# Idle products of ones ahead of product 0, and the second direction's buckets, counts and ranks spread over products 5 to 15

## The reference

```python
x = x + gnn(layernorm(x), src, dst, edge_type)     # x: 625 x 512
x = x + moe(layernorm(x))

def gnn(input, heads, tails, rel):                  # W_rel: 16 x 512 x 512
    h_self = input @ W_self.T + b_self
    H_all = einsum('rod,nd->rno', W_rel, input) + b_rel[:, None, :]
    agg = segment_sum(H_all[rel, tails], heads) + segment_sum(H_all[rel + 8, heads], tails)
    return relu(h_self + agg)

def moe(x):                                         # gate, up: 16 x 512 x 1024, down: 16 x 1024 x 512
    top_vals, top_idx = top_k(x @ router_w.T, 2)
    # per expert: (silu(x @ gate) * (x @ up)) @ down, weighted by the softmax of top_vals
```

## Time and profile before

| what | value |
|---|---|
| median of 3 runs | 710.33 us (709.69 to 710.6) |
| profiled execution, its own time | 708.9 us |
| its span, first to last instruction | 706.7 us |
| TensorE busy in the span | 683.2 us, 97% |
| VectorE busy | 607.1 us, 86% |
| ScalarE busy | 499.5 us, 71% |
| GpSimd busy | 293.1 us, 41% |
| mean granted TensorE clock | 0.994 |

### The profile page before, as it was taken

The page is one execution under the profiler, slowest core; times in us unless marked ns, Lnnn a source line. Parts: engine busy times, 40 slices in busy tenths (PEclk is TensorE's granted clock), DMA queues, the critical chain, the costliest instruction groups (busy, mean ns, idle before and its releaser), DMA issues. The chain is left out here.

```text
span 706.7 us, 10496 instructions
## 1 busy us (share of the span) xinstructions
PE 683.2 (97%) x3196; PEld 541.4 (77%) x3196; DVE 607.1 (86%) x1193; ACT 499.5 (71%) x712; POOL 293.1 (41%) x255
## 2 busy tenths in 40 slices
PE   4899999999999999999998989999999999999996
PEld 4677777777777777787766867888888888888884
DVE  8789979998999777775766989999998999999982
ACT  5645458775777777777556759888887877887881
POOL 3000037874777777757750034332231322333301
PEclk9999999999999999999998999999999999999999
DMA  7358579897999999986779699999999999999952
GB/s 254 111 164 277 149 224 333 289 286 252 317 282 301 306 308 303 303 293 210 211 214 328 257 346 403 406 405 395 407 364 406 373 374 377 359 387 376 354 190 31
DMA packets 60170, 210.69 MB, mean 298 GB/s; under 512 B 9325, under 2 KB 9722, under 8 KB 47070
## 3 DMA queue, kind: packets, MB, share of 16 engines
q1 hardware_dynamic: 41534, 154.43, 58.2%
q0 software_dynamic: 18592, 55.73, 27.4%
HBM read 181.83 MB, written 28.29 MB: 297 GB/s over the span
## 5 line engine op out<-in xcount | busy, mean ns | idle before, releaser
L416 POOL DMA_INDIRECT rows_sb<-h_dram,row_of x180 | 201.8, 1121 | 156.6 <-DVE row_of L574 89.2
L584 DVE TENSOR_TENSOR rows_lo<-rows_sb,rows_hi 128x512 fp32r<-128x512 f32 x165 | 112.8, 684 | 31.6 <-ACT rows_hi L728 31.4
L871 PE MATMUL p_h<-g_hi_sb,xt_hi_whole 128*125 128x512 f32 x320 | 128.4, 401 | 0.8 <-DVE xt_lo_whole L501 0.5
L872 PE MATMUL p_h<-g_lo_sb,xt_hi_whole 128*125 128x512 f32 x320 | 126.9, 396 | 0.0
L873 PE MATMUL p_h<-g_hi_sb,xt_lo_whole 128*125 128x512 f32 x320 | 126.7, 396 | 0.0
L728 ACT CAST rows_hi<-rows_sb 128x512 fp32r<-128x512 f32 x165 | 97.5, 617 | 22.4 <-DMA rows_sb<-h_dram,row_of 21.2
L715 ACT COPY h_whole<-p_h 125x512 f32<-125x512 f32 x80 | 46.8, 585 | 81.8 <-PE p_h L873 77.6
L1250 POOL DMA_INDIRECT tokens<-token_dram,rows_of_tokens x15 | 21.2, 1416 | 173.9 <-ACT rows_of_tokens L1556 133.8
L1304 DVE TENSOR_TENSOR u_lo_sb<-stage_up,u_hi_sb 128x2048 fp32r<-128x2048 f32 x34 | 76.4, 2285 | 1.1
L1304 DVE TENSOR_TENSOR d_lo_sb<-stage_down,d_hi_sb 128x2048 fp32r<-128x2048 f32 x32 | 71.9, 2287 | 3.7 <-ACT d_hi_sb L1541 3.7
L1678 PE MATMUL p_gate<-g_hi_sb,xt_lo_whole 128*128 128x512 f32 x256 | 74.1, 400 | 0.0
(11 more groups left out here) (308 smaller groups left out, 1304.2 us busy)
## 6 DMA issues: line engine op xcount, KB each, us to landing
stage_up<-in_L_ffn_up_w SPq DMA_DIRECT2D x34, 1024.0 KB, 8.7
stage_gate<-in_L_ffn_gate_w SPq DMA_DIRECT2D x32, 1024.0 KB, 8.7
stage_down<-in_L_ffn_down_w SPq DMA_DIRECT2D x32, 1024.0 KB, 8.4
h_dram<-h_whole SPq DMA_DIRECT2D x80, 256.0 KB, 4.1
stage_up<-in_L_gnn_W_rel SPq DMA_DIRECT2D x64, 256.0 KB, 5.5
x_whole<-in_biases SPq DMA_DIRECT2D x16, 256.0 KB, 6.4
rows_sb<-h_dram,row_of POOLq DMA_INDIRECT x180, 5.2
stage_gate<-in_L_ffn_down_w SPq DMA_DIRECT2D x2, 1024.0 KB, 10.1
```

Of the source, the lines that this page charges most:

```text
L416: q.indirect_dma_start(rows_sb[:, b % ROWS], None, h_dram[0:1 + made(n) * P], bass.IndirectOffsetOnAxis(ap=row_of[:, column_of[b]:column_o ...
L584: v.tensor_tensor(rows_lo[:, b % PARTS], rows_sb[:, b % ROWS], rows_hi[:, b % PARTS].bitcast(F32), ALU.subtract).then_inc(part_lo, 1)
L871: m.matmul(o, xt_hi[:, dc, at], wt_hi_sb[:, 1 - j % 2, dc], start=(by_matmul and dc == 0), stop=False, skip_group_check=True)
L872: m.matmul(o, xt_hi[:, dc, at], wt_lo_sb[:, 1 - j % 2, dc], start=False, stop=False, skip_group_check=True)
```

## The change

It does five things.

1. A function `keep_going(n)` issues n matmuls of the 128 by 128 tile of ones with itself into a bank of `p_h` that nobody reads before product 1 overwrites it. Five stand in the first block, seven ahead of `totals_of(0)`, two behind `ranks(0)` and three behind `turn_x(1)`.
2. `turn_x(2)`, `turn_x(3)` and `turn_x(4)` stand inside products 1, 2 and 3, behind the second of the four pieces, instead of inside products 1 and 2 behind the third and after product 2.
3. ScalarE takes the bias and the later tiles' roots earlier, VectorE the bias, tile 2's statistics and product 1's operands.
4. Direction 1's steps move: on VectorE `buckets_of(1)` and `bucket_hots(1)` from behind `scales(1)` to behind `places(0)`, `totals_of(1)` into product 7, `spans_begin` from 3 to 9, `ranks(1)` from 5 to 12, `ranks(2)` from 7 to 15; on TensorE `totals_of(1)` behind product 5, the counts behind 8, `ranks(1)` behind 10, `ranks(2)` behind 13. Totals and counts get columns in `p_sum` in place of `p_list`.
5. The marks move from products 10 to 14 to products 16 to 20.

```diff
--- before.py
+++ after.py
@@ -47,6 +47,7 @@
 LISTS = ((5, 5.5), (25, 3))
 
 LAG, START, PACE = 4, 25, 3.0
+MARKS = 16
 
 LAST_HOTS, ROUTER = 56, 72
 LOW, BIASES = 32, 2 * R + 1
@@ -263,8 +264,8 @@
             p_logits = p_list[0:TP, 0:T * NX].rearrange("p (t e) -> p t e", t=T)
             p_router = p_list[:, 256:256 + NX]
             p_ranks = p_sum[:, 0:3]
-            p_totals = [p_list[0:EC, 0:2 * T], p_list[0:EC, 2 * T:BUCKETS]]
-            p_counts = p_list[0:EXTRA + 1, 128:128 + BUCKETS]
+            p_totals = [p_list[0:EC, 0:2 * T], p_sum[0:EC, 4, 0:BUCKETS - 2 * T]]
+            p_counts = p_sum[0:EXTRA + 1, 3, 0:BUCKETS]
 
 
             PARTS_OF = ((0, 0, 2), (1, 2, 5), (1, 5, 6))
@@ -319,6 +320,11 @@
             def token_columns(a, t):
 
                 return a[:, :, t * TP:(t + 1) * TP]
+
+            def keep_going(n):
+
+                for _ in range(n):
+                    nc.tensor.matmul(p_h[:, 1, 0:P], ones[:], ones[:], start=True, stop=True)
 
             def turned(t):
                 return p_sum[:, 3 + t % 2, 0:KC * TP].rearrange("p (c n) -> p c n", c=KC)
@@ -617,42 +623,43 @@
                 normal(1)
                 scales(0)
                 scales(1)
-                buckets_of(1)
-                bucket_hots(1)
+                dve.wait_ge(bias_hi, 1)
+                v.tensor_tensor(bias_parts[LOW:LOW + BIASES], bias_f[LOW:LOW + BIASES], bias_parts[LOW:LOW + BIASES].bitcast(F32),
+                                ALU.subtract).then_inc(bias_ready, 1)
+                dve.wait_ge(rest_loaded, 16)
+                normal(2)
                 low_columns(0)
                 for dc in range(KC):
                     w_rest(0, dc)
                 low_columns(1)
-                dve.wait_ge(bias_hi, 1)
-                v.tensor_tensor(bias_parts[LOW:LOW + BIASES], bias_f[LOW:LOW + BIASES], bias_parts[LOW:LOW + BIASES].bitcast(F32),
-                                ALU.subtract).then_inc(bias_ready, 1)
-                totals_of(1)
-                dve.wait_ge(rest_loaded, 16)
-                normal(2)
                 scales(2)
                 normal(3)
+                ranks(0)
                 scales(3)
                 low_columns(2)
-                ranks(0)
                 normal(4)
                 low_columns(3)
                 scales(4)
                 told_of(0)
-                dve.wait_ge(ranks_taken, 1)
-                places(0)
                 low_columns(4)
                 for dc in range(KC):
                     w_rest(1, dc)
+                dve.wait_ge(ranks_taken, 1)
+                places(0)
+                buckets_of(1)
+                bucket_hots(1)
                 dve.wait_ge(edge_consts, 2)
                 for i in range(PRODUCTS):
                     j, t = i // T, i % T
                     if j and t:
                         w_rest(j + 1, t - 1)
-                    if i == 3:
+                    if i == 7:
+                        totals_of(1)
+                    if i == 9:
                         spans_begin()
-                    if i == 5:
+                    if i == 12:
                         ranks(1)
-                    if i == 7:
+                    if i == 15:
                         ranks(2)
                         dve.wait_ge(ranks_taken, 3)
                         then(v.tensor_tensor(place_in[:, 1], place_in[:, 1], rank_part[:], ALU.max))
@@ -756,21 +763,21 @@
                     s.activation(rstd[:, t:t + 1], rstd[:, t:t + 1], ACT.Sqrt).then_inc(root_ready, 1)
 
                 first_root(0)
+                act.wait_ge(bias_loaded, 16)
+                s.copy(bias_parts[:], bias_f[:]).then_inc(bias_hi, 1)
                 first_root(1)
                 scaled(0)
                 scaled(1)
                 turned_high(0)
+                first_root(2)
                 for dc in range(KC):
                     w_main(0, dc)
                 turned_high(1)
-                act.wait_ge(bias_loaded, 16)
-                s.copy(bias_parts[:], bias_f[:]).then_inc(bias_hi, 1)
-                take(0)
-                first_root(2)
                 scaled(2)
                 first_root(3)
+                take(0)
+                bias_in(2)
                 turned_high(2)
-                bias_in(2)
                 scaled(3)
                 take(1)
                 bias_in(3)
@@ -794,8 +801,8 @@
                     take(i)
                     if i + 2 < PRODUCTS:
                         bias_in(i + 2)
-                    if 10 <= i < 10 + T:
-                        carry_in(i - 10)
+                    if MARKS <= i < MARKS + T:
+                        carry_in(i - MARKS)
                     for b in blocks[PARTS - 3:]:
                         message(b)
                 act.wait_ge(gate_loaded, 32)
@@ -872,7 +879,7 @@
                         m.matmul(o, xt_hi[:, dc, at], wt_lo_sb[:, 1 - j % 2, dc], start=False, stop=False, skip_group_check=True)
                         last = m.matmul(o, xt_lo[:, dc, at], wt_hi_sb[:, 1 - j % 2, dc], start=False, stop=False,
                                         skip_group_check=True)
-                        if dc == KC - 2 and turned is not None:
+                        if dc == 1 and turned is not None:
                             turn_x(turned)
                     if i == 0:
                         pe.wait_ge(bias_ready, 1)
@@ -943,24 +950,28 @@
                     if t == T - 1:
                         i.then_inc(self_done, 1)
 
+                keep_going(7)
                 totals_of(0)
                 pe.wait_ge(totals_ready, 1)
                 ranks(0)
+                keep_going(2)
                 turn_x(0)
                 turn_x(1)
-                totals_of(1)
+                keep_going(3)
                 for i in range(PRODUCTS):
-                    if 10 <= i < 10 + T:
-                        mark(i - 10)
-                    product(i, i + 1 if i in (1, 2) else None)
-                    if i == 2:
+                    if MARKS <= i < MARKS + T:
+                        mark(i - MARKS)
+                    product(i, i + 1 if i in (1, 2, 3) else None)
+                    if i == 5:
+                        pe.wait_ge(xt_ready, T)
+                        totals_of(1)
+                    if i == 8:
                         pe.wait_ge(totals_ready, 2)
                         m.matmul(p_counts, ones16[0:EC, 0:EXTRA + 1], totals[0:EC], start=True, stop=True).then_inc(counts_full, 1)
-                        turn_x(4)
-                    if i == 4:
+                    if i == 10:
                         pe.wait_ge(totals_ready, 5)
                         ranks(1)
-                    if i == 6:
+                    if i == 13:
                         ranks(2)
                     for d in range(2):
                         for n in chunks(d, i):
@@ -1022,6 +1033,11 @@
                     q.tensor_tensor(select[:], ident[:, 0:BIASES], ident[:, LOW:LOW + BIASES], ALU.add)
                     q.tensor_scalar(big16[:], ident[0:EP, 0:EP], BIG, None, ALU.mult).then_inc(consts_ready, 1)
                     pool.wait_ge(consts_ready, 4)
+
+                @block.tensor
+                def _(pe):
+                    pe.wait_ge(consts_ready, 2)
+                    keep_going(5)
 
                 @block.scalar
                 def _(act):
```

## The result

| | before | after |
|---|---|---|
| median of 13 executions each | 710.33 us (708.08 to 711.27) | 708.65 us (706.92 to 710.69) |
| profiled execution, its own time | 708.9 us | 708.17 us |
| its span | 706.7 us | 706.1 us |

The ratio after to before is 0.9976, 95% interval 0.9965 to 0.9988: 1.7 us faster. The forecast was 707.0 (706.0 to 710.5): right in sign, inside the range, 1.65 us too hopeful. The two profiled executions differ by only 0.7 us, less than the medians do, and both numbers need an explanation.

The account below looks back on a forecast made before the run. TensorE, busy every microsecond from 100 to 300 us, paces the rest; its first 30 us are loose. 5.15 - 0.65 - 0.9 - 0.05 - 0.1 = 3.45, less 0.2: 3.3 us off the median 710.33, so 707.0 (706.0 to 710.5).

Parts of the forecast that it names:

- case-B: Start-up: clock rises between ranks(0) and product 0; gain 2.4 to 1.5 us, time 707.9 to 708.8; chance 0.22.
- case C: Start-up: idle products don't raise the clock before product 0; nothing gained, 710.4 us; chance 0.25.
- case A: Start-up: clock high from ranks(0) on, product 0 starts at 13.9; 3.3 us gained, 707.0 us; chance 0.45.
- the weights' landing: ScalarE's weight casts before product 0: the last weight piece may land late, up to 0.5 us; 0.2 taken off.
- my other bound: Length of one idle product at the low clock by the transposes' spacing: 0.48 us, not the 0.43 taken.
- the five in the first block: First five idle products, ending at about 4.25 us: cost 0 to 0.3 us, taken as 0.05.
- the seven are covered: Seven idle products from 4.6 to 7.6 us, before the buckets TensorE waits for until 7.91: no cost.
- no wait is left ahead of `turn_x(4)`: Products 2 and 3: tile 4 is normalised at 24.65, before turn_x(4) at 24.95; waits of 0.55 and 1.82 us go.
- ScalarE holds product 4: TensorE idles 1.7 us ahead of product 4 for ScalarE's p_h copy; product 4 starts at 28.4.
- VectorE the totals: Behind product 5, totals_of(1) waits 0.65 us for VectorE's buckets, done at 34.7.
- rival D: Products 7 to 15: VectorE late for the list, slower; 1.5 us beyond its lead gives 712; chance 0.08.
- Found again at 300 us: Dense part: the 3 us gained at product 6 should still be there at 300 us, or the prediction is wrong.

Follow-up runs that it names:

- e3: Kernel before with only the 17 idle products added, in the old order of steps; 709.68 us, ratio 0.9984.
- e11: Changed kernel with product 4's bias earlier on ScalarE, totals_of(1) behind product 6, and no idle products ahead of product 0; 707.22 us, ratio 0.9958.
- e9: Changed kernel with product 4's bias earlier, no two idle products behind ranks(0), totals_of(1) behind product 6; 706.92 us, ratio 0.9955 (5 executions).
- e2: Changed kernel without its 17 idle products ahead of product 0; 708.55 us, ratio 0.9975.
- e1: Control: changed kernel with only the waits on the number of rounds written as constants; 708.29 us, ratio 0.9963.
- e5: Changed kernel with fourteen more idle products around the last router logits, between the layers; 709.77 us, ratio 0.9999.
- e10: Control again: changed kernel with only the waits on rounds as constants, run beside e9; 708.57 us, ratio 0.9974 (9 executions).
- e7: Changed kernel with TensorE's totals_of(1) behind product 6 instead of 5; 706.97 us, ratio 0.9975.
- e8: Same kernel as e9, an earlier set of executions; 706.33 us, ratio 0.9949.
- e6: Changed kernel without the two idle products behind ranks(0); 707.95 us, ratio 0.9973.
- e4: Changed kernel with ScalarE's take(2) and bias_in(4) ahead of relation 1's last two weight casts; 708.7 us, ratio 0.9972.
- e12: Kernel before with only the four waits on the number of rounds written as constants; 709.74 us, ratio 0.9994.

## Why the forecast came out as it did

**The sign was right; how much of it the idle products earn is open.** They go with an earlier rise of the clock: product 0 takes 3.08 to 3.37 us in all ten traces with them, and 4.57, 4.64, 4.68 and 3.10 in the four without. Where product 0 would otherwise run at the low clock, they are worth 1.1 to 2.1 us at product 25 in the old order (e3's 102.20 against 103.34 and 104.30) and 1.56 in the new one (e11 against e9). Where it would not, as in e2's trace, they cost: product 25 starts at 101.23 there, and at 101.80 to 102.01 in the case-B traces with all 17. In the times only e3 shows them alone (1.15 us). In the new order, without them (e2), 1.83 of the 2.26 us that e1 gains by the means are left, while case C had "nothing" for the new order at the low clock. Either e2's executions mostly have the early rise, or C was priced too low; no trace has the changed order alone with a slow product 0.

**The step that failed is the chance of case A.** I gave A 0.45, B 0.22 and C 0.25. Of the four traces that run the changed kernel up to the layers' boundary (after, e1, e5, e10), one is A and three are B; with all kernels that hold idle products, four of ten are A (e1, e3, e7, e8), six are B, none is C. B was priced at a gain of 2.4 to 1.5, with product 0 at 14.8 if the clock is up right behind `ranks(0)` and at 15.6 if it rises only at the last three idle products. In the trace after, it is up by the transposes, but the two idle products ahead of them still take 0.99 us; product 0 starts at 15.42, and the lead at product 25 is 1.45, 1.33 and 1.54, about the lower end. B was the commoner case, and 708.8 its upper number; the median is 708.65. That the two agree so well is in part luck: the forecast let the lead reach the end whole, and in the trace after only 0.6 of 1.45 us does. The rule of the Trainium skill that I had cited with C (TensorE: Matmul & The Clock Gate, Part 1, the point of the rise varies between runs) deserved more: the traces agree with it, `ranks(0)` taking 2.51 us in one execution and 1.32 in another.

**Case A itself was about 0.5 too large.** e1 leads by 2.73 us at product 25, where the sum was 3.25 with 0.2 kept back for the weights' landing. The weights cost nothing: ScalarE's casts begin at 12.65 without a wait. The 0.2 goes elsewhere: VectorE's first `w_rest` begins at 13.29, as forecast, but product 0, which it releases, starts at 14.12 instead of 13.9. Product 4 starts at 29.06 instead of 28.4: VectorE's `scales(4)` stands behind `low_columns(3)`, which itself waits for ScalarE until 23.38, so tile 4 is normalised at 25.2 instead of 24.65. I had that chain 0.4 too short.

**An idle product** takes 0.495 us at the low clock and 0.22 at the high one (three in 0.67, from 373.48 to 374.15 in e5). I had taken 0.43 for the low clock; my other bound, 0.48 by the transposes, was the better one. That is 0.99 instead of 0.86 for the two, and e6 shows that 0.64 of it delays product 0 in case B.

**Right as written:** the five in the first block cost 0.05 (`ranks(0)` at 9.10 instead of 9.05); the seven are covered; no wait is left ahead of `turn_x(4)`; ScalarE holds product 4 and VectorE the totals; `totals_of(1)` costs 0.82 us (0.9 forecast); rival D, VectorE late for the list, is not there: no wait for a list chunk in the trace after. e4 shows how near VectorE is: one microsecond more of lead turns into a wait of 1.8 for its buckets, and in that execution the clock falls.

**"Found again at 300 us" held mostly, but not to the end.** In nine of the thirteen traces beside that of before, the lead or lag at product 25 is there at product 75 within 0.02 us. The trace after loses 0.19, e9 0.50, e11 0.78 and e1 1.22 us (2.73 to 1.51), so in e1, the one case A of the control, nearly half was not found again. Most of e1's loss is where ScalarE waits for a transfer of fetched rows, VectorE for ScalarE, and TensorE for VectorE:

```profile
152.84 0.62 ACT L735 CAST rows_hi<-rows_sb 128x512 fp32r<-128x512 f32 x1 [1.67 <-DMA rows_sb<-h_dram,row_of]
...
156.13 0.69 DVE L590 TENSOR_TENSOR rows_lo<-rows_sb,rows_hi 128x512 fp32r<-128x512 f32 x1 [0.78 <-ACT rows_hi L735]
...
156.87 0.50 PE L914 MATMUL p_sum<-rows_hi,seg_hot 128*125 128x512 f32 x1 [0.42 <-DVE rows_lo L590]
```

In the trace after the lead was 1.26 at product 75 and at the last turn. Then it went in two steps. First, the block between the layers. VectorE's copy of the logits and its first instruction of layer 2, in e12 (order of before):

```profile
378.02 0.24 DVE L689 COPY logits<-p_list 125x80 f32<-125x80 f32 x1 [0.33 <-PE p_list L930]
379.54 0.07 DVE L1300 MEMSET mask<- 125x8 uint32 x1 [1.28 <-PEq L1064]
```

and in the changed kernel:

```profile
376.12 0.24 DVE L696 COPY logits<-p_list 125x80 f32<-125x80 f32 x1 [0.66 <-PE p_list L937]
377.90 0.07 DVE L1316 MEMSET mask<- 125x8 uint32 x1 [1.55 <-PEq L1080]
```

The wait at the boundary is 1.28 us in the three traces of the old order (before, e3, e12) and 1.54 or 1.55 in the ten of the new one that leave it untouched, with or without idle products. So 0.26 us go with the new order, each time; e5 alone alters the place. Another 0.4 of the trace after goes at the logits' copy, whose wait is 0.66 us there and 0.24 in the trace before; it varies from one trace to the next (e10 has no such wait). Second, the low clock of the first microseconds of layer 2:

```profile
378.00:379.00 1.00, 1.00 (x3) 0.68 (x3) 0.90 (x4) 0.97 (x2) 0.00 (x0) 0.55 0.16 55
...
384.00:385.00 1.00, 1.00 (x4) 0.75 (x4) 0.86 (x5) 0.00 (x0) 0.00 (x0) 0.54 1.02 270
385.00:386.00 1.00, 1.00 (x6) 0.73 (x5) 0.22 (x1) 0.59 (x1) 0.00 (x0) 1.00 0.79 299
```

Before:

```profile
384.00:385.00 1.00, 1.00 (x6) 0.82 (x5) 0.87 (x4) 0.05 (x1) 0.00 (x0) 0.94 1.08 344
385.00:386.00 1.00, 1.00 (x6) 0.73 (x5) 0.81 (x4) 0.59 (x1) 0.00 (x0) 1.00 0.93 258
```

The low stretch is 6.8 us long in both, but it begins at 377.3 in the trace before, 1.3 us ahead of layer 2, and at 378.1 in the trace after, 0.1 behind its start. So more of layer 2's work met the low clock. From the last turn to the third tokens the two traces of before take 40.65 and 40.43 us, the three of the changed kernel 41.92, 44.09 and 41.37, e9 40.93, e11 41.26. e1's 44.09 has a wait of 3.51 us for the tokens' transfer, which is 1.71 in the trace after, and a low stretch of 10.2 us, until 386.5:

```profile
384.00:386.00 2.00, 2.00 (x7) 1.54 (x6) 1.20 (x5) 0.65 (x2) 0.00 (x0) 0.50 0.94 269
...
417.61 1.12 PE L1705 MATMUL p_x<-ident,tokens 128*128 128x128 f32 x4 [3.51 <-DMA tokens<-token_dram,rows_of_tokens]
```

The length of the low stretch sorts all fourteen traces. Where it is 6.8 us (before, e3, e12, after, e9, e10, e11), the way from layer 2's start to the third tokens takes 36.1 to 37.0 us; where it is 10.2 (e1, e2, e4, e6, e7, e8), 37.4 to 37.9, and 39.6 in e1; where it is 3.4 (e5), 35.6. The three traces of the old order all have 6.8; of the ten of the new one that leave the boundary alone, four have 6.8 and six 10.2. Of the lead at the end of the span in the trace after, 0.6 us, all came back behind the third tokens.

**What stays open.** Why the boundary costs 0.26 us more in the new order; whether the longer low stretch belongs to that order or to the executions that were profiled (none of three traces against six of ten); why the clock rises early in one execution and late in the next; how much of the median gain the idle products earn. What e11 gives up at product 1 is in its trace, but not in its median; with six executions it can't be told whether others of its executions have the early rise, as e2's had.

## What to carry to other kernels

Matmuls that fill a loose start to raise the clock pay only for what would have run at the low clock, here about 1.5 us of one product, and nothing in an execution whose clock rises in time without them. The moment of the rise differs between executions: a forecast should price every such case and weigh them nearly alike, not take the best. A test without the idle products must keep the rest of the change, or the order's own gain is credited to them. When a chain in a start-up is shortened, look at the next engine that is late, and take its wait in the same step: alone, e4 gained nothing; together with the later totals and without the two idle products it gave 1.6 us. And carry a lead through to the last instruction: a boundary between two parts of a program can take half of it.

## What the runs showed of the hardware

- The granted clock reads 1.00 from 0 to 30 us both in the trace before and in that of e11, where matmuls of 512 columns follow each other at 0.43 us; by e12's record it falls at 16 us and reads 0.50 to 19 us, where their spacing agrees. In these traces the first stretch of the column can't be trusted.
- The clock fell in the middle of dense work in e4, behind a wait of 1.80 us and 20 one-column matmuls: the record reads 0.50 from 38 to 44 us. Behind the wait of 0.77 and the same matmuls in the changed kernel it did not. One trace shows it, and not that the wait is the cause.
- A 4-byte matmul of 128 columns leaves two records and takes 0.495 us at the low clock, 0.22 at the high one, that is more than the 0.43 and 0.21 which a quarter of the 512-column 4-byte matmul of the earlier trace rows would give.
